# Slot arithmetic and scale vectors of y on GpSimd instead of VectorE, in a four-block Flamingo kernel

## What is computed

```python
x = x + tanh(g_xattn[0]) * memory_block(ctx, layernorm(x))       # shifted rows and a short convolution
x = x + tanh(g_ffn[0])   * (fp6_blocks(layernorm(x)) @ fp6_blocks(W).T + bias)
x = x + tanh(g_xattn[1]) * attention(layernorm(x), ctx, key_mask)
x = x + tanh(g_ffn[1])   * moe(layernorm(x))

def moe(t):                                   # 8 experts, cap = 1280 tokens each
    probs = softmax(t @ Wr); idx = argmax(probs); pmax = max(probs)
    pos  = (running count of the token within its expert) - 1
    kept = pos < cap
    eout = relu(t_at_slot @ W1[e]) @ W2[e]    # each kept token in slot idx*cap + pos
    return where(kept, eout * pmax, t)
```

## Time and profile before

| | us |
|---|---|
| Runs, median of 3 | 2067.8 (2064.79 to 2069.31) |
| The profiled execution's own time | 2065.28 |
| Its span in the trace | 2063.5 |
| TensorE busy | 1927.6 (93%) |
| VectorE busy | 964.2 (47%) |
| GpSimd busy | 757.6 (37%) |
| ScalarE busy | 742.2 (36%) |

### The profile page before, as it was taken

The page is one execution under the profiler, slowest core; times in us unless marked ns, Lnnn a source line. Parts: engine busy times, 40 slices in busy tenths (PEclk is TensorE's granted clock), DMA queues, the critical chain, the costliest instruction groups (busy, mean ns, idle before and its releaser), DMA issues.

```text
span 2063.5 us, 34727 instructions
## 1 busy us (share of the span) xinstructions
PE 1927.6 (93%) x10956; PEld 1637.0 (79%) x10957; DVE 964.2 (47%) x2254; ACT 742.2 (36%) x1707; POOL 757.6 (37%) x803
## 2 busy tenths in 40 slices
PE   3579999999999739999999999999999999999997
PEld 2467777777777538989889988998898898899986
DVE  3678999999996571423312241224224124122331
ACT  2235666666566531423311141114214114111231
POOL 0456566675664231423311151115215115211340
PEclk9589999999999869999999999999999999999999
DMA  7231453443544381433401152004305115200220
GB/s 199 93 94 42 142 178 119 167 136 125 182 133 161 106 284 31 145 96 94 130 30 30 36 167 66 30 30 153 98 25 173 36 36 168 77 30 30 81 82 11
DMA packets 152268, 208.77 MB, mean 101 GB/s; under 512 B 12830, under 2 KB 78622, under 8 KB 152197
## 3 DMA queue, kind: packets, MB, share of 16 engines
q1 hardware_dynamic: 111125, 114.14, 17.8%
q0 software_dynamic: 15728, 43.38, 7.0%
q10 hardware_dynamic: 25344, 50.33, 6.8%
HBM read 140.98 MB, written 68.37 MB: 101 GB/s over the span
## 4 chain that ended last, share of the span: by engine, by line
PE 78%; DVE 6%; issue 5%; DVEq 1%; DMA 1%; ACT 1%; POOL 1%; SPq 0%; ACTq 0%; POOLq 0%
PE bank L788 25%; PE bank L796 24%; PE bank L1483 7%; PE bank L1405 6%; PE bank L756 6%; PE bank L736 6%; PE bank L1455 1%; DVE x2T_lo L1803 1%; PE bank L714 1%; PE bank L745 1%; DVE xdT_lo L1803 1%; DMA stage<-in_L_ffn_W_dram 1%; PE bank L1413 1%; DVE up_lo L1794 1%; DVE a_m L1899 0%
## 5 line engine op out<-in xcount | busy, mean ns | idle before, releaser
L896 DVE SCALAR_TENSOR_TENSOR hT_lo<-bank,hT_hi 128x256 fp32r<-128x256 f32 x352 | 149.2, 424 | 676.9 <-ACT hT_hi L664 676.9
L664 ACT ACTIVATE hT_hi<-bank 128x256 fp32r<-128x256 f32 x352 | 134.9, 383 | 753.9 <-PE bank L788 753.9
L788 PE MATMUL bank<-inT_hi,w_hi 128*128 128x256 f32 x1408 | 399.7, 284 | 0.6 <-DVEq L944 0.6
L788 PE MATMUL bank<-inT_hi,w_lo 128*128 128x256 f32 x1408 | 400.0, 284 | 0.0
L788 PE MATMUL bank<-inT_lo,w_hi 128*128 128x256 f32 x1408 | 396.7, 282 | 0.0
L796 PE MATMUL bank<-w_hi,hT_hi 128*128 128x512 f32 x704 | 280.8, 399 | 0.0
L796 PE MATMUL bank<-w_lo,hT_hi 128*128 128x512 f32 x704 | 277.9, 395 | 0.0
L788 PEld LDWEIGHTS bank<-inT_lo,w_hi 128*128 128x128 f32 x1408 | 266.3, 189 | 14.5
L796 PE MATMUL bank<-w_hi,hT_lo 128*128 128x512 f32 x704 | 277.6, 394 | 0.0
L788 PEld LDWEIGHTS bank<-inT_hi,w_hi 128*128 128x128 f32 x1408 | 266.0, 189 | 13.9 <-DVEq L944 1.0
L788 PEld LDWEIGHTS bank<-inT_hi,w_lo 128*128 128x128 f32 x1408 | 265.2, 188 | 0.0
(11 more groups left out here) (314 smaller groups left out, 3830.5 us busy)
## 6 DMA issues: line engine op xcount, KB each, us to landing
stage<-in_L_ffn_W_dram SPq DMA_DIRECT2D x256, 256.0 KB, 3.2
X<-in_x_dram SPq DMA_DIRECT2D x16, 1024.0 KB, 5.5
t_d<-tt ACTq DMA_DIRECT2D x16, 1024.0 KB, 4.4
x_d<-x ACTq DMA_DIRECT2D x16, 1024.0 KB, 6.7
out_dram<-y ACTq DMA_DIRECT2D x16, 1024.0 KB, 8.4
xs<-in_x_dram SPq DMA_DIRECT2D x16, 768.0 KB
cw_a<-in_L_xattn_conv_w_dram SPq DMA_DIRECT2D x2, 1024.0 KB, 17.8
cw_b<-in_L_xattn_conv_w_dram SPq DMA_DIRECT2D x2, 1024.0 KB, 19.9
```

What stands on the lines that cost most here:

```text
L664: act.activation(hT_hi[:, f % 4, :], hb[f % 4][:, 0:CN], ACT.Relu).then_inc(e_hh, 1)
L788: last = pe.matmul(hb[f % 4][:, 0:CN], l[:, k, fs], r[:, k, :], start=(n == 0), stop=(n == 3 * KB - 1))
L896: dve.scalar_tensor_tensor(out=hT_lo[:, f % 4, :], in0=hb[f % 4][:, 0:CN], scalar=0.0, in1=hT_hi[:, f % 4, :].bitcast(F32), op0=ALU.max, o ...
```

## The change

In `scatter_slots(g)` GpSimd now computes the slots itself, in a `slots_of(g)` of its own: eleven instructions, with `fl3` as a new tile, and waits on two new semaphores of its own (`g_sl`, `g_pay`). On VectorE `posi` and `posm` (a bitwise and) stay and move into `positions()`; the rest of `slots_of` is gone. `y_of(g)` computes `y_sc` and `y_nb` on GpSimd, ahead of y, once `nb_d` is there (`g_ys`). VectorE waits for GpSimd before it writes `pos`, `rp`, `rwm` and `nb_d` again. The other edits renumber waits on `v_pp` and `v_ys`.

```diff
         def _(pool):
             def scatter_slots(g):
-                wait(pool, v_flat, g + 1)
+                slots_of(g)
+                wait(pool, g_pay, 4 * g + 4)
                 settled(pool)
                 for j in range(T):
                     pool.indirect_dma_start(
...
+            def slots_of(g):
+                wait(pool, v_pp, 4 * g + 4)
+                wait(pool, s_slot, 16 * T * g)
+                settled(pool)
+                pool.tensor_scalar(over[:, :], pos[:, :], float(CAP), float(1 << 20), ALU.is_gt, ALU.mult).then_inc(g_sl, 1)
+                pool.tensor_scalar(fl1[:, :], rwm[:, :], -float(CT), float(E * CT) - 1.0 / P, ALU.mult, ALU.add).then_inc(g_sl, 1)
+                pool.tensor_scalar(fl2[:, :], pos[:, :], 1.0 / P, None, ALU.mult).then_inc(g_sl, 1)
+                pool.tensor_scalar(fl3[:, :], posm[:, :], NC - 1.0 / P, None, ALU.mult).then_inc(g_sl, 1)
+                wait(pool, g_sl, 7 * g + 4)
+                pool.tensor_tensor(over[:, :], over[:, :], fl1[:, :], ALU.add).then_inc(g_sl, 1)
+                pool.tensor_tensor(fl2[:, :], fl2[:, :], fl3[:, :], ALU.add).then_inc(g_sl, 1)
+                wait(pool, v_re, 3 * g + 3)
+                pool.tensor_scalar(pay[:, :, 1], rp[:, :], gates[:, 3:4], None, ALU.mult).then_inc(g_pay, 1)
+                pool.tensor_copy(pay[:, :, 0].bitcast(I32), tokid[:, :]).then_inc(g_pay, 1)
+                wait(pool, g_sl, 7 * g + 6)
+                pool.tensor_tensor(fl2[:, :], fl2[:, :], over[:, :], ALU.add).then_inc(g_sl, 1)
+                wait(pool, g_sl, 7 * g + 7)
+                pool.tensor_copy(flat[:, :], fl2[:, :]).then_inc(g_pay, 1)
+                wait(pool, g_pay, 4 * g + 3)
+                pool.tensor_scalar(tokid[:, :], tokid[:, :], float(G), None, ALU.add).then_inc(g_pay, 1)
+
             def y_of(g):
-                wait(pool, v_ys, 3 * (g + 1))
+                wait(pool, v_ys, g + 1)
+                wait(pool, a_rs["d"], 2 * (g + 1))
+                settled(pool)
+                pool.tensor_scalar(y_sc[:, :], rs_d[:, :], gates[:, 3:4], 1.0, ALU.mult, ALU.add).then_inc(g_ys, 1)
+                pool.tensor_scalar(y_nb[:, :], nb_d[:, :], gates[:, 3:4], None, ALU.mult).then_inc(g_ys, 1)
+                wait(pool, g_ys, 2 * g + 2)
                 wait(pool, s_y, 16 * g)
...
-            def slots_of(g):
-                wait(dve, v_pp, 7 * g + 2)
-                dve.tensor_scalar(over[:, :], ...
-                dve.tensor_scalar(posi[:, :], ...
-                dve.scalar_tensor_tensor(out=fl1[:, :], in0=rwm[:, :], ...
-                wait(dve, v_pp, 7 * g + 5)
-                dve.scalar_tensor_tensor(out=fl2[:, :], in0=fl1[:, :], ...
-                dve.tensor_scalar(posm[:, :], posi[:, :], ...
-                wait(dve, v_pp, 7 * g + 7)
-                dve.scalar_tensor_tensor(out=fl1[:, :], in0=posm[:, :], ...
-                wait(dve, v_fl, g + 1)
-                wait(dve, s_slot, 16 * T * g)
-                wait(dve, v_re, 3 * g + 3)
-                wait(dve, v_tok, g)
-                dve.tensor_scalar(pay[:, :, 1], rp[:, :], ...
-                dve.tensor_copy(pay[:, :, 0].bitcast(I32), tokid[:, :])...
-                dve.tensor_scalar(flat[:, :], fl1[:, :], ...
-                wait(dve, v_pay, 2 * g + 2)
-                dve.tensor_scalar(tokid[:, :], tokid[:, :], ...
...
# positions()
                     dve.tensor_tensor(rpe[:, :, :], p_pos[:, :, :], oh[:, :, :], ALU.mult).then_inc(v_pp, 1)
-                    wait(dve, v_pp, 7 * e + 1)
+                    wait(dve, v_pp, 4 * e + 1)
+                    wait(dve, g_sl, 7 * e)
+                    settled(dve)
                     dve.tensor_reduce(pos[:, :], rpe[:, :, :], AX.X, ALU.add).then_inc(v_pp, 1)
+                    wait(dve, v_pp, 4 * e + 2)
+                    dve.tensor_scalar(posi[:, :], pos[:, :], -1.0, None, ALU.add).then_inc(v_pp, 1)
+                    wait(dve, v_pp, 4 * e + 3)
+                    dve.tensor_scalar(posm[:, :], posi[:, :], P - 1, None, ALU.bitwise_and).then_inc(v_pp, 1)
...
# scale_of_y()
+                    wait(dve, g_y, T * e)
+                    settled(dve)
                     if late(e):
                         wait(dve, a_tt, T * e)
-                        wait(dve, g_y, T * e)
...
-                    dve.tensor_scalar(y_sc[:, :], rs_d[:, :], gates[:, 3:4], 1.0, ALU.mult, ALU.add).then_inc(v_ys, 1)
-                    wait(dve, v_ys, 3 * e + 1)
-                    dve.tensor_scalar(y_nb[:, :], nb_d[:, :], gates[:, 3:4], None, ALU.mult).then_inc(v_ys, 1)
...
# routed()
+                    wait(dve, g_pay, 4 * e)
+                    settled(dve)
                     dve.reciprocal(rp[:, :], rsum[:, :]).then_inc(v_re, 1)
-                    slots_of(e)
...
# the router's chain, ahead of rwm
                     wait(dve, v_r, 7 * d + 5)
+                    wait(dve, g_sl, 7 * d)
+                    settled(dve)
                     dve.tensor_reduce(rwm[:, :], rw[:, :, :], AX.X, ALU.max).then_inc(v_r, 1)
```

More of the change, by code:

```diff
@@ L177, in flamingo_two_layers @@
         s_xs, s_x, s_uq, s_cx, s_t, s_x3, s_y, s_slot = (sem("s_" + n) for n in ("xs", "x", "uq", "cx", "t", "x3", "y", "slot"))
-        g_u, g_x1, g_xb, g_xd, g_y = (sem("g_" + n) for n in ("u", "x1", "xb", "xd", "y"))
+        g_u, g_x1, g_xb, g_xd, g_y, g_sl, g_pay, g_ys = (sem("g_" + n) for n in ("u", "x1", "xb", "xd", "y", "sl", "pay", "ys"))
         a_n1, a_bh, a_sq, a_ch, a_uh, a_st, a_al, a_th, a_tt, a_sd, a_re, a_mc, a_md, a_lt = (
@@ L190, in flamingo_two_layers @@
         v_sm, v_scf, v_tl, v_x3, v_ys, v_la, v_re = (sem("v_" + n) for n in ("sm", "scf", "tl", "x3", "ys", "la", "re"))
-        v_r, v_oh, v_pp, v_fl, v_pay, v_tok, v_flat = (sem("v_" + n) for n in ("r", "oh", "pp", "fl", "pay", "tok", "flat"))
+        v_r, v_oh, v_pp = (sem("v_" + n) for n in ("r", "oh", "pp"))
         LN = 2 * T + 1
@@ L331, in flamingo_two_layers @@
         lq = small("lq", T, 4, E)
+        fl3 = small("fl3", T)
         def convolved(eng):
@@ L1288, in body @@
                 if e is not None:
-                    wait(act, v_ys, 3 * e + 1)
+                    wait(act, v_ys, e + 1)
                     wait(act, s_t, 16 * e)
@@ L1475, in project @@
                         if e is not None:
-                            wait(pe, v_pp, 7 * e + 1)
+                            wait(pe, v_pp, 4 * e + 1)
                     if h >= 2:
@@ L1671, in shift @@
                                          op0=ALU.mult, op1=ALU.mult).then_inc(v_ln[kind], 1)
-            def slots_of(g):
-                wait(dve, v_pp, 7 * g + 2)
-                dve.tensor_scalar(over[:, :], pos[:, :], float(CAP), float(1 << 20), ALU.is_gt, ALU.mult).then_inc(v_pp, 1)
-                dve.tensor_scalar(posi[:, :], pos[:, :], -1.0, None, ALU.add).then_inc(v_pp, 1)
-                dve.scalar_tensor_tensor(out=fl1[:, :], in0=rwm[:, :], scalar=-float(CT * P), in1=pos[:, :],
-                                         op0=ALU.mult, op1=ALU.add).then_inc(v_pp, 1)
-                wait(dve, v_pp, 7 * g + 5)
-                dve.scalar_tensor_tensor(out=fl2[:, :], in0=fl1[:, :], scalar=1.0 / P, in1=over[:, :],
-                                         op0=ALU.mult, op1=ALU.add).then_inc(v_pp, 1)
-                dve.tensor_scalar(posm[:, :], posi[:, :], P - 1, None, ALU.bitwise_and).then_inc(v_pp, 1)
-                wait(dve, v_pp, 7 * g + 7)
-                dve.scalar_tensor_tensor(out=fl1[:, :], in0=posm[:, :], scalar=NC - 1.0 / P, in1=fl2[:, :],
-                                         op0=ALU.mult, op1=ALU.add).then_inc(v_fl, 1)
-                wait(dve, v_fl, g + 1)
-                wait(dve, s_slot, 16 * T * g)
-                wait(dve, v_re, 3 * g + 3)
-                wait(dve, v_tok, g)
-                dve.tensor_scalar(pay[:, :, 1], rp[:, :], gates[:, 3:4], None, ALU.mult).then_inc(v_pay, 1)
-                dve.tensor_copy(pay[:, :, 0].bitcast(I32), tokid[:, :]).then_inc(v_pay, 1)
-                dve.tensor_scalar(flat[:, :], fl1[:, :], float(E * CT) - 1.0 / P, None, ALU.add).then_inc(v_flat, 1)
-                wait(dve, v_pay, 2 * g + 2)
-                dve.tensor_scalar(tokid[:, :], tokid[:, :], float(G), None, ALU.add).then_inc(v_tok, 1)
             def late(g):
```

## The result

The changed kernel takes 2072.68 us (median of 7 runs, 2070.86 to 2076.81); the kernel before, in 7 runs beside it, 2066.91 (2064.79 to 2069.31). The ratio is 1.0028, with a 95% interval of 1.0016 to 1.0039: the change makes the kernel slower, by 5.8 us, where 6.4 us less was predicted, and the time lies above the range. The profiled execution took the median itself, 2072.68 us, with a span of 2071.0, 7.5 us longer than before.

A forecast was written before the change was run, and what follows sets the result against it. TensorE and VectorE are nearly full, with VectorE's tail paced by GpSimd. -5.0 us over eleven rounds and -1.4 in the last rounds make -6.4: 2058.9 us profiled, 2061 against the median; range 2052 to 2071.

The forecast's parts named there:

- What bounds the round: TensorE's for two thirds of a round, then VectorE's last third, paced by GpSimd; TensorE's waits hold 1.8 us a round.
- the 1.0 at most: Most counted per round, in us, if VectorE reaches the later adds one GpSimd instruction sooner; TensorE's waits cap it.
- VectorE's middle: Mid-round, moved work leaves VectorE: `q` ends 1.1 us earlier, worth nothing to TensorE, which its own matmuls cover.
- GpSimd's arithmetic: Ahead of the scatters: slots take 3.3 us, `y` starts 0.35 us later, first scatter at 442.3 instead of 440.46.
- the 0.45 us: GpSimd's `n` and the adds after it start this much earlier, shortening each of 11 rounds by as much.
- Rival 3: Scatters starved beside `q`: each of four waits 0.6 us, shift +2.0, 2058 us; far longer starving over 2130; chance 0.05.
- what a shift does to the tail: VectorE's small tail instructions end with a GpSimd add; from -0.75 to +0.5 us the period changes by the shift.
- the tooth at +0.5: Above this GpSimd shift in us, VectorE gets in one add sooner; the period falls by about 1.45 minus the shift.
- the forecast -5.0: Predicted change in us over the eleven rounds having both the moved work and the tail: 11 x 0.45.
- The last rounds: In the round at 713 us `alT_lo` no longer waits behind the slots' arithmetic: 1.4 us won.
- the handoff: After the last group: GpSimd needs 1.9 us more, stores go 2 us earlier; put at nothing, -2 to +2 us.
- The slower rival: Scatters end so late that TensorE waits for `n`, from a shift of 2.9 us on: 2084 us; chance 0.14 with milder relatives.

The follow-up runs named there:

- the kernel with the split and the wait: Kernel before, two of four `gbias` adds moved behind the scaling of `xs`, a wait for their results behind them: 2054.19 us, ratio 0.9955.
- the first experiment: Changed kernel plus one GpSimd wait for its own four `n` results, ahead of the `gbias` adds: 2060.72 us, ratio 0.9975.

## Why the prediction was wrong

- **What bounds the round: right.** The end of VectorE's tail, paced by GpSimd's adds, sets the period. In the kernel with the split and the wait the end of `a_sc` lies 1.4 us earlier, and the round takes 36.07 us, a gain of 1.1, near the 1.0 at most that I had counted.
- **VectorE's middle: right.** `q` ends 12.2 us after `alT_lo`, before 13.0: 0.8 to 0.9 us earlier, I had taken 1.1. It was worth nothing by itself, as said.
- **GpSimd's arithmetic: too short.** The slots took 3.56 us from the end of `y` to the first scatter (3.3 taken), and `y` itself was 0.62 us late (0.35 taken): the scatter starts 2.37 us later, not 1.84. Small instructions take 0.18 to 0.33 us here, not 0.155. That alone ate the 0.45 us: s, the shift of GpSimd's sequence, is -0.05 where no scatter is stretched.
- **Scatters beside q: a rival, and it came in part.** Rival 3 put 0.6 us on each of four. Measured: 0.5 us on none, one or two, so s is -0.05, +0.47 or +0.98. The rule of the Trainium skill, SBUF — State Buffer, section "SBUF: two separate sides", that was weighed there (620 ns becoming some 3100 beside a VectorE copy) doesn't appear at its size: beside the product `q`, of 0.68 us each, 0.97 us becomes 1.49.
- **The step that failed** is the one taken for certain in "what a shift does to the tail": that a small VectorE instruction gets in at the end of the GpSimd instruction that runs. By it +0.98 would have gained 1.45 - 0.98 = 0.47 us, as the first experiment shows for +0.72 (36.35 us a round), and -0.05 and +0.47, below the tooth at +0.5, would have moved the round by as much: 3 x -0.05 + 5 x 0.47 - 3 x 0.47 = 0.8 us lost in eleven rounds. So of the 14.1 us between the forecast -5.0 and the measured +9.1, 5.8 come from s and 8.3 from this step. The rows of before show it only behind a pause: ahead of `n` in the earlier trace rows stand 2.46 us of waiting. The change takes that pause away, and `a_m` is held to the end of the whole run of adds. I had counted the lost pause as free, and even as the gain.
- **The last rounds and the handoff: right in kind.** `alT_lo` is no longer late, and 1.1 us were gained for 1.4 predicted, but not where I had them: 0.27 us in the round of the late `alT_lo` and 0.87 in the one before it, at another granted clock. That the sum comes near is in part luck; the kernel before with the wait behind `n` has the same code in these two rounds, and they took 65.85 us there (granted clock 0.95 and 0.80) against 63.13 (0.95 and 0.93). The handoff gave 0.5, within -2 to +2.
- **The slower rival** named the wrong place: TensorE never waits for `n`. Slower came from below s = 2.9, by the tail.

The Trainium skill, GPSIMD Engine Reference, has a box by which consecutive GpSimd instructions are no barrier between its eight cores, while an instruction counts as complete once all are done.
## What to carry to other kernels

Where VectorE's small instructions meet a run of long GpSimd instructions, look at what stands ahead of the run: a pause there may be what lets VectorE in between, and work that fills it isn't free. When such an instruction takes two or three GpSimd instructions' time, try a wait for GpSimd's own results right ahead of the run (0.20 us here) before anything else is moved. And order the two engines so that they don't meet in the tail: two adds behind the scaling of `xs`, and that wait, in the kernel before, made it 2054.19 us, 0.45% faster than before, and left TensorE as the bound; moving work off VectorE added nothing to it.

## What the hardware showed that was not expected

- VectorE's two-input instruction or cast of 128x4 or 128x8 elements can be held over several GpSimd instructions: 2.0 to 3.0 us for `a_m`, 3.6 to 4.1 us for `cntb`, always to the end of the run. With a wait for own results right ahead of the run the same instructions waited for the running one alone; a stop of 1.1 to 2.3 us some six instructions earlier didn't save `cntb`.
- A scatter's issue on GpSimd takes 0.97 us alone, and 1.48 to 1.51 us in some of the rounds in which it runs beside `q`. Each meeting costs one of the two: in the changed kernel, from its second of the eleven rounds on, in rounds with no stretched scatter two of the four `q` instructions take 0.73 to 0.75 us, with one stretched scatter one does, and with two none (0.68 us each).
- Small GpSimd instructions of 128x4 elements take 0.18 to 0.33 us, and an indirect DMA's issue starts 0.86 us after the end of the one that it waits for.
